# DLRM tower on one core: the opening's index casts, table differences and one-hots in a new order

## The chip, the cores and the metric

The kernel runs on one core of one Trainium2 chip. The metric is the device time of one execution in microseconds, as the median of several runs.

## What is computed

For 2048 samples, 40 embedding rows of 32 values are looked up. Every pair of fields (780 pairs) gets its own 32x32 matrix, and the value of the pair is the bilinear form of the two rows. The 780 values and 16 dense values then go through three dense layers.

```python
e = jnp.stack([tbl_0[ids[:, 0]], tbl_1[ids[:, 1]], ...], axis=1)   # 40 tables of 1000 to 125000 rows
xi = inputs[:, iidx, :]
xj = inputs[:, jidx, :]
out = jnp.einsum('bpd,pde,bpe->bp', xi, bilinear_matrices, xj)
h = jnp.concatenate([z, dense_ctx], axis=1)
h = jnp.maximum(h @ W_top1 + b_top1, 0.0)
h = jnp.maximum(h @ W_top2 + b_top2, 0.0)
y = h @ W_top3
```

## The kernel before

The batch is cut into four blocks of 512 samples. The fields stand in ten chunks of four, and the work of a block is 50 units (a chunk against a chunk, or against itself). A cycle `g` of the main loop is one unit: `project` multiplies a chunk by its matrices on TensorE into the PSUM tile `U` (two halves), `multiply` takes the product with the other chunk on VectorE, and `sum_up` adds over the 32 values on TensorE into `bank_z`. Between these, each cycle carries a few pieces of other work on TensorE (`MISC_AT`): lookups of a coming block, or the dense layers of the last one.

Most fields (24 of 40 in the first two blocks, 28 in the others) are gathered from HBM by GpSimd (`rows`, L589) and turned by a TensorE transpose (L914). The other fields, sixteen in the first two blocks and all of small tables, are looked up without a gather, in four groups of four fields (`GROUPS`, numbered 0 to 3, used in the order 0, 1, 3, 2). A lookup `look(o, q, k)` of block `o` and group `q` has ten steps `k`: VectorE compares the indices with a row number and writes a one-hot tile (`one_hot`, L792), and TensorE multiplies it by that part of the table, 12 matmuls per step, into `misc` (L891). The one-hots live in a ring of five (`ONES`), so that step n+5 waits for TensorE's step n. When ten steps are done, ScalarE copies `misc` away (`keep_look`, L645).

Two things must be made ready for that:

- **Tables.** Each table is split into three bf16 parts. For a group `q`, ScalarE writes the high part (`split_hi`, L606), VectorE the difference (`split_rest`, L772), ScalarE the middle part (`split_mid`, L613), VectorE the last part (`split_low`, L779); each in two halves. `look` waits for the last part.
- **Indices.** The one-hot needs the indices of the group spread over 125 partitions (`idx_wide`, two buffers, jobs alternating). For block 0, group 0, TensorE spreads them by products with an identity (L1004), and ScalarE copies them (L691). For all the others, TensorE turns all 16 index columns (L1012), ScalarE copies them as `idx_T` (L699) and stores them in HBM (`idx_rows`, L702), and the SP queue reads them back to all 125 partitions (`load_wide`, L498).

The SP queue is one list in order of the program. After the index store it reads back the indices of group 1, loads the matrices of step 2 (`load_W(2)`), the tables of group 2, the indices of group 3, `load_W(3)`, the indices of group 2, `load_W(4)` and so on. It stands behind one wait for the store:

```python
sp.wait_ge(idx_stored, 16)
load_wide(0, 1)
load_W(2)
for f in GROUPS[2]:
    load_tab(sp, 2, f)
load_wide(0, 3)
load_W(3)
load_wide(0, 2)
```

Every engine has its own program in order, written by hand; nothing is scheduled by a tool. "The opening" is what runs before the main loop: lookups of groups 0, 1 and 3, and the first two gathered chunks. A program's order of the instructions is fixed, and the engines meet by semaphores alone.

## Time and profile before

| what | value |
|---|---|
| median of 3 runs | 728.96 us (727.7 to 730.28) |
| the profiled execution's own time | 728.67 us |
| its span in the trace | 726.9 us |
| TensorE busy | 693.9 us, 95% of the span |
| VectorE busy | 597.1 us, 82% |
| GpSimd busy | 522.2 us, 72% |
| ScalarE busy | 197.1 us, 27% |

The span is the stretch between the first and the last instruction of the trace; the execution's own time is 1.8 us more. The busy shares are averages over stages with different limits, so the opening has to be read in its own stretches.

### The profile page before, as it was taken

All of it is one profiled execution on the core that took longest, in us unless ns stands there. A gap on an engine that the chain in (4) does not pass through costs nothing.

```text
span 726.9 us, 15700 instructions
## 1 busy us (share of the span) xinstructions
PE 693.9 (95%) x6512; PEld 215.8 (30%) x6512; DVE 597.1 (82%) x608; ACT 197.1 (27%) x309; POOL 522.2 (72%) x631
## 2 busy tenths in 40 slices
PE   2767999999999999999999999999999999999998
PEld 2233333332332232322332232322332222222232
DVE  7989999999986989979876998979967878787800
ACT  3344411422052113043142103143143012213102
POOL 7888888888887888888887888888888887830000
PEclk9999999999999999999999999999999999999999
DMA  4555351222004020000004020000001000000000
GB/s 126 111 89 86 60 99 40 58 52 43 12 12 71 12 40 13 11 12 13 12 12 71 12 35 18 11 12 12 12 12 16 12 12 12 12 8 1 1 1 1
DMA packets 62692, 22.77 MB, mean 31 GB/s; under 512 B 46287, under 2 KB 61805, under 8 KB 62621
## 3 DMA queue, kind: packets, MB, share of 16 engines
q1 hardware_dynamic: 49277, 14.86, 8.8%
q0 software_dynamic: 13312, 6.84, 8.2%
q8 instruction: 51, 0.84, 0.5%
q14 instruction: 20, 0.16, 0.1%
q10 hardware_dynamic: 32, 0.07, 0.1%
HBM read 21.65 MB, written 0.07 MB: 30 GB/s over the span
## 4 chain that ended last, share of the span: by engine, by line
PE 89%; DVE 5%; ACT 4%; DMA 1%; issue 1%; ACTq 0%; DVEq 0%
PE U L940 28%; PE bank_z L965 26%; PE misc L992 14%; PE misc L891 10%; PE U L992 4%; PE U L949 3%; DVE ones L792 3%; PE U L914 3%; ACT x_T L645 1%; DMA idx_wide<-idx_rows 1%; DVE prod L828 1%; ACT x_twin L663 1%; PE bank_z L973 0%; DVE tabs L779 0%; ACT x_twin L666 0%
## 5 line engine op out<-in xcount | busy, mean ns | idle before, releaser
L589 POOL DMA_INDIRECT rows<-in_tbl,idx x416 | 410.2, 986 | 121.3 <-issue 63.5
L828 DVE TENSOR_TENSOR prod<-U,x_T 128x1024 f32<-128x1024 f32 x280 | 329.5, 1216 | 56.5 <-PE U L940 53.7
L965 PE MATMUL bank_z<-prod,select 128*32 128x512 f32 x1600 | 213.1, 604 | 0.7 <-ACT z L625 0.7
L940 PE MATMUL U<-x_T,W 32*128 32x512 f32 x1184 | 187.0, 640 | 7.4 <-ACT x_T L636 3.6
L792 DVE TENSOR_SCALAR ones<-idx_wide,row_of 125x2048 bf16<-125x2048 f16 x140 | 119.0, 872 | 7.0 <-ACT idx_wide L691 3.4
L891 PE MATMUL misc<-ones,tabs 125*32 125x512 bf16 x1680 | 108.4, 388 | 7.3 <-DVE ones L792 5.3
L597 POOL MEMSET pause<- 128x448 uint8 x208 | 111.7, 537 | 0.1
L828 DVE TENSOR_TENSOR prod<-U,x_look 128x1024 f32<-128x1024 f32 x80 | 94.3, 1218 | 21.0 <-PE U L940 18.5
L992 PE MATMUL misc<-z,W 128*32 128x512 f32 x728 | 92.0, 592 | 0.0
L940 PEld LDWEIGHTS U<-x_T,W 32*128 32x128 f32 x1184 | 57.8, 183 | 102.9 <-issue 49.4
L636 ACT ACTIVATE x_T<-U 32x512 f32<-32x512 f32 (+2 forms) x48 | 28.3, 591 | 188.8 <-PE U L914 115.0
L965 PEld LDWEIGHTS bank_z<-prod,select 128*32 128x32 f32 x1600 | 31.6, 107 | 153.5 <-issue 81.4
L891 PEld LDWEIGHTS misc<-ones,tabs 125*32 125x32 bf16 x1680 | 47.4, 98 | 85.0 <-issue 46.0
L625 ACT ACTIVATE z<-bank_z 128x512 f32<-128x512 f32 x28 | 16.7, 598 | 115.8 <-PE bank_z L965 98.7
L940 PE MATMUL U<-x_look,W 32*128 32x512 f32 x256 | 41.8, 640 | 0.0
L645 ACT ACTIVATE x_T<-misc 32x512 f32<-32x512 f32 (+1 forms) x36 | 21.2, 589 | 68.1 <-PE misc L891 67.7
L992 PEld LDWEIGHTS misc<-z,W 128*32 128x32 f32 x728 | 23.6, 110 | 52.7 <-issue 52.7
L992 PE MATMUL misc<-h,W 128*32 128x512 f32 (+1 forms) x204 | 30.4, 593 | 0.8 <-ACT x_T L645 0.8
L663 ACT ACTIVATE x_twin<-x_T 32x512 f32<-32x512 f32 x48 | 30.1, 627 | 1.2
L680 ACT ACTIVATE h<-misc,b 128x512 f32<-128x512 f32 x13 | 8.9, 688 | 64.3 <-PE misc L992 64.3
L949 PE MATMUL U<-x_T,W 32*64 32x512 f32 x160 | 24.1, 612 | 1.2 <-ACT x_twin L673 1.2
L816 DVE TENSOR_TENSOR prod<-U,x_twin 128x1024 f32<-128x1024 f32 x20 | 24.3, 1214 | 0.0
(67 smaller groups left out, 284.1 us busy)
## 6 DMA issues: line engine op xcount, KB each, us to landing
rows<-in_tbl,idx POOLq DMA_INDIRECT x416
idx_wide<-idx_rows SPq DMA_DIRECT2D x13, 500.0 KB
W<-in_W_top SPq DMA_DIRECT2D x100, 8.0 KB
W<-_L_rec_bilinear_matrices SPq DMA_DIRECT2D x72, 16.0 KB, 3.2
prod<-in_tbl SPq DMA_DIRECT2D x4, 156.2 KB
W<-in_W_top SPq DMA_DIRECT2D x35, 2.0 KB
W<-_L_rec_bilinear_matrices SPq DMA_DIRECT2D x4, 128.0 KB
W<-in_W_top SPq DMA_DIRECT2D x1, 512.0 KB
```

The source lines that it names most:

```text
L589: nc.gpsimd.indirect_dma_start(out=rows[:, n % R_SLOTS, t, f, :], out_offset=None, in_=tables[field][:, :], in_offset=bass.IndirectOffsetO ...
L597: nc.gpsimd.memset(pause[:], 0).then_inc(paused, 1)
L636: last = nc.scalar.activation(x_of(o, J)[lo * DIM:hi * DIM, :], U[lo * DIM:hi * DIM, at, 0:N], ACT.Copy)
L645: last = nc.scalar.activation(x_of(o, J)[lo * DIM:hi * DIM, :], misc[s * DIM:(s + hi - lo) * DIM, 0:ROWS[o]], ACT.Copy)
L663: nc.scalar.activation(x_twin[r * DIM:(r + 1) * DIM, 1, 0:N], x_of(o, a + 1)[(CF - 1 - r) * DIM:(CF - r) * DIM, :], ACT.Copy)
L792: nc.vector.tensor_scalar(ones[:, n % ONES, 0:len(fs), 0:N], idx_wide[job % 2][:, 0:len(fs), 0:N], row_of[0:KP, k:k + 1], None, ALU.is_equ ...
L828: last = nc.vector.tensor_tensor(to[:, :, m * N:(m + n) * N].rearrange("p r (m n) -> p r m n", m=n), U[:, at:at + 2, m * N:(m + n) * N].re ...
L891: last = nc.tensor.matmul(misc[s * DIM:(s + 1) * DIM, 0:N], tabs[0:KP, LOOKED.index(field), part, k * DIM:(k + 1) * DIM], ones[:, n % ONES ...
L940: last = nc.tensor.matmul(U[:, at + r % 2, m * N:(m + 1) * N], W[row, at_W:at_W + P], x_of(o, a)[row, :], start=True, stop=True, skip_grou ...
L949: last = nc.tensor.matmul(U[side * P // 2:(side + 1) * P // 2, at + r % 2, m * N:(m + 1) * N], W[row, at_W + side * P // 2:at_W + (side + ...
L965: last = nc.tensor.matmul(bank_z[r * DIM:(r + 1) * DIM, 0:N], sel, prod[:, (2 * g + r // 2) % P_SLOTS, r % 2, m * N:(m + 1) * N], start=(k ...
L992: last = nc.tensor.matmul(bank[part, 0:N], lhs[:, part], rhs, start=(t == 0), stop=(t == depth - 1), skip_group_check=True)
```

## The change

Only the opening changes; no instruction is of a new kind. The indices of group 1 are spread by products on TensorE as those of group 0 are (16 more matmuls and one more copy on ScalarE), and no longer read back from HBM (one SP transfer less). For that, four small casts instead of one stand at the head of VectorE's list, ahead of a memset of `rows`. VectorE makes two one-hots, then the difference of group 0's tables, then the others; the differences of group 3 come behind all ten one-hots of group 1. TensorE turns the 16 index columns after four steps of the first lookup, not ahead of it, so that the copy `idx_T` and the store come after the table copies of group 1. ScalarE zeroes `dense` later, and copies group 3's middle part after `keep_look(0, 1)`, not ahead of it.

```diff
@@ -525,7 +525,6 @@
             for f in GROUPS[3]:
                 load_tab(sp, 3, f)
             sp.wait_ge(idx_stored, 16)
-            load_wide(0, 1)
             load_W(2)
             for f in GROUPS[2]:
                 load_tab(sp, 2, f)
@@ -690,22 +689,24 @@
             act.wait_ge(wide_full, 1)
             nc.scalar.activation(idx_wide[0][:], U[0:KP, 2:2 + CF, :], ACT.Copy).then_inc(wide_made, 1)
 
-            nc.scalar.activation(dense[:].rearrange("p t r d -> p t (r d)"),
-                                 ident[:].unsqueeze(1).to_broadcast([P, SUBS, P]), ACT.Copy, scale=0.0
-                                 ).then_inc(dense_zeroed, 1)
             split_hi(0)
             split_mid(0)
+            act.wait_ge(wide_full, 2)
+            nc.scalar.activation(idx_wide[1][:], U[0:KP, 2:2 + CF, :], ACT.Copy).then_inc(wide_made, 1)
+            split_hi(1)
+            split_mid(1)
             act.wait_ge(idx_T_full, 1)
             nc.scalar.activation(idx_T, U[0:NL, 0:BATCH // NB, :].rearrange("p b n -> p (b n)"), ACT.Copy
                                  ).then_inc(idx_T_made, 1)
             act.wait_ge(idx_T_made, 1)
             act.dma_start(idx_rows[:, :], idx_T).then_inc(idx_stored, 16)
-            split_hi(1)
-            split_mid(1)
+            nc.scalar.activation(dense[:].rearrange("p t r d -> p t (r d)"),
+                                 ident[:].unsqueeze(1).to_broadcast([P, SUBS, P]), ACT.Copy, scale=0.0
+                                 ).then_inc(dense_zeroed, 1)
             keep_look(0, 0)
             split_hi(3)
+            keep_look(0, 1)
             split_mid(3)
-            keep_look(0, 1)
             split_hi(2)
             for g in range(-2, G + 1):
                 if g == 4:
@@ -748,9 +749,6 @@
             nc.vector.tensor_copy(ident_h[:], ident[:]).then_inc(ident_h_made, 1)
             dve.wait_ge(row_of_made, 1)
             nc.vector.tensor_copy(row_of[:], row_of_i[:]).then_inc(row_of_f_made, 1)
-            nc.vector.memset(rows[:, 1:5], 0.0).then_inc(rows_zeroed, 1)
-
-
             beside = [(LOOKED.index(f), f, n) for f, n in ((36, 4), (0, 1), (24, 1), (2, 2), (16, 1), (9, 1), (34, 1),
                                                            (23, 1), (28, 1), (22, 1), (30, 1), (27, 1))]
 
@@ -760,7 +758,8 @@
                 return last
 
             dve.wait_ge(ids_loaded, 16)
-            to_half(0, ROWS[0] // P, beside[:1]).then_inc(idx_h_made, 1)
+            to_half(0, ROWS[0] // P, beside[:4]).then_inc(idx_h_made, 1)
+            nc.vector.memset(rows[:, 1:5], 0.0).then_inc(rows_zeroed, 1)
             for a in range(0, CHUNKS, 2):
                 zero = nc.vector.memset(W[:, w_col(a, a):w_col(a, a) + P], 0.0)
             zero.then_inc(W_zeroed, 1)
@@ -783,10 +782,10 @@
                 N, fs = ROWS[o], GROUPS[q]
                 n, job = LOOK_PART[(o, q, k)], LOOK_ORDER.index((o, q))
                 if k == 0:
-                    if job == 0:
-                        dve.wait_ge(wide_made, 1)
+                    if job < 2:
+                        dve.wait_ge(wide_made, job + 1)
                     else:
-                        dve.wait_ge(wide_landed[job % 2], 16 * ((job + 1) // 2))
+                        dve.wait_ge(wide_landed[job % 2], 16 * (job // 2))
                 if n >= ONES:
                     dve.wait_ge(ones_used, n - ONES + 1)
                 nc.vector.tensor_scalar(ones[:, n % ONES, 0:len(fs), 0:N], idx_wide[job % 2][:, 0:len(fs), 0:N],
@@ -833,32 +832,31 @@
                 last.then_inc(multiplied, 1)
 
             dve.wait_ge(row_of_f_made, 1)
-            for k in range(ONES):
+            for k in range(2):
                 one_hot(0, 0, k)
+            split_rest(0)
+            one_hot(0, 0, 2)
+            split_low(0)
+            one_hot(0, 0, 3)
+            split_rest(1)
             dve.wait_ge(ids_rest_loaded, 16)
-            to_half(ROWS[0] // P, BATCH // P, beside[:1])
-            to_half(0, BATCH // P, beside[1:]).then_inc(idx_h_rest_made, 1)
-            split_rest(0)
-            split_low(0)
-            for k in range(ONES, KC):
+            to_half(ROWS[0] // P, BATCH // P, beside[:4])
+            to_half(0, BATCH // P, beside[4:]).then_inc(idx_h_rest_made, 1)
+            for k in range(4, KC):
                 one_hot(0, 0, k)
-                if k == ONES + 1:
-                    split_rest(1)
-                if k == ONES + 3:
+                if k == 5:
                     split_low(1)
             nc.vector.memset(select[:], 0.0).then_inc(select_zeroed, 1)
             nc.vector.memset(rows[:, 5:7], 0.0).then_inc(rows_zeroed, 1)
             for k in range(KC):
                 one_hot(0, 1, k)
-                if k == ONES:
-                    split_rest(3)
-                if k == ONES + 2:
-                    split_low(3)
+            split_rest(3)
             dve.wait_ge(select_zeroed, 1)
             for s in range(CF):
                 at = CF * (UPT - 1) + s
                 last = nc.vector.memset(select[s * DIM:(s + 1) * DIM, at:at + 1], 1.0)
             last.then_inc(constants, 1)
+            split_low(3)
             for n in HOT_AT[-2]:
                 one_hot(*LOOK_OF_PART[n])
             split_rest(2)
@@ -999,21 +997,25 @@
             pe.wait_ge(ident_h_made, 1)
             pe.wait_ge(idx_h_made, 1)
 
-            for s in range(CF):
-                for t in range(ROWS[0] // P):
-                    last = nc.tensor.matmul(U[0:KP, 2 + s, t * P:(t + 1) * P],
-                                            idx_h[:, t, s:s + 1].to_broadcast([P, KP]), ident_h[:],
-                                            start=True, stop=True, skip_group_check=True)
-            last.then_inc(wide_full, 1)
-            for t in range(BATCH // P):
-                if t == 0:
-                    pe.wait_ge(idx_h_rest_made, 1)
+            for q in (0, 1):
+                if q:
                     pe.wait_ge(wide_made, 1)
-                last = nc.tensor.matmul(U[0:NL, t // SUBS, t % SUBS * P:(t % SUBS + 1) * P], idx_h[:, t, :], ident_h[:],
-                                        start=True, stop=True, skip_group_check=True)
-            last.then_inc(idx_T_full, 1)
+                for s in range(CF):
+                    for t in range(ROWS[0] // P):
+                        last = nc.tensor.matmul(U[0:KP, 2 + s, t * P:(t + 1) * P],
+                                                idx_h[:, t, CF * q + s:CF * q + s + 1].to_broadcast([P, KP]), ident_h[:],
+                                                start=True, stop=True, skip_group_check=True)
+                last.then_inc(wide_full, 1)
             for q in (0, 1):
                 for k in range(KC):
+                    if (q, k) == (0, 4):
+                        pe.wait_ge(idx_h_rest_made, 1)
+                        pe.wait_ge(wide_made, 2)
+                        for t in range(BATCH // P):
+                            last = nc.tensor.matmul(U[0:NL, t // SUBS, t % SUBS * P:(t % SUBS + 1) * P],
+                                                    idx_h[:, t, :], ident_h[:], start=True, stop=True,
+                                                    skip_group_check=True)
+                        last.then_inc(idx_T_full, 1)
                     look(0, q, k)
             pe.wait_ge(constants, 1)
             pe.wait_ge(idx_T_made, 1)
```

The order of VectorE's instructions at the start of its program. `prod`, `W` and `h` are the memory in which the tables of groups 0 and 1, 3, and 2 are staged; `select` is a constant. Before:

```order
L750 CAST row_of<-row_of_i 128x10
L751 MEMSET rows 128x2048
L759 CAST idx_h<-idx 128x4x4
L765 MEMSET W 128x128 x5
L792 TENSOR_SCALAR ones<-idx_wide,row_of 125x2048 x5
L759 CAST idx_h<-idx 128x12x4
L759 CAST idx_h<-idx 128x16 x2
L759 CAST idx_h<-idx 128x16x2
L759 CAST idx_h<-idx 128x16 x8
L772 TENSOR_TENSOR prod<-prod,tabs 125x4x160 x2
L779 TENSOR_TENSOR tabs<-prod,tabs 125x4x160 x2
```

And of the change:

```order
L751 CAST row_of<-row_of_i 128x10
L757 CAST idx_h<-idx 128x4x4
L757 CAST idx_h<-idx 128x4 x2
L757 CAST idx_h<-idx 128x4x2
L762 MEMSET rows 128x2048
L764 MEMSET W 128x128 x5
L791 TENSOR_SCALAR ones<-idx_wide,row_of 125x2048 x2
L771 TENSOR_TENSOR prod<-prod,tabs 125x4x160 x2
L791 TENSOR_SCALAR ones<-idx_wide,row_of 125x2048
L778 TENSOR_TENSOR tabs<-prod,tabs 125x4x160 x2
L791 TENSOR_SCALAR ones<-idx_wide,row_of 125x2048
```

The memset moved behind the first casts, and the difference and the last part of group 0 moved ahead of the third and the fourth one-hot.

The order of ScalarE's instructions from its first copy to the middle part of group 2's tables. The destination `h` is `idx_T`, `tabs<-W` is group 3 and `tabs<-h` is group 2. Before:

```order
L691 ACTIVATE idx_wide<-U 125x2048
L693 ACTIVATE dense<-ident 128x512
L606 ACTIVATE tabs<-prod 125x4x160 x2
L613 ACTIVATE tabs<-prod 125x4x160 x2
L699 ACTIVATE h<-U 16x2048
L702 DMA idx_rows<-h 16x2048
L606 ACTIVATE tabs<-prod 125x4x160 x2
L613 ACTIVATE tabs<-prod 125x4x160 x2
L645 ACTIVATE x_look<-misc 128x512
L606 ACTIVATE tabs<-W 125x4x160 x2
L613 ACTIVATE tabs<-W 125x4x160 x2
L645 ACTIVATE x_T<-misc 32x512 x2
```

And of the change:

```order
L690 ACTIVATE idx_wide<-U 125x2048
L605 ACTIVATE tabs<-prod 125x4x160 x2
L612 ACTIVATE tabs<-prod 125x4x160 x2
L695 ACTIVATE idx_wide<-U 125x2048
L605 ACTIVATE tabs<-prod 125x4x160 x2
L612 ACTIVATE tabs<-prod 125x4x160 x2
L699 ACTIVATE h<-U 16x2048
L702 DMA idx_rows<-h 16x2048
L703 ACTIVATE dense<-ident 128x512
L644 ACTIVATE x_look<-misc 128x512
L605 ACTIVATE tabs<-W 125x4x160 x2
L644 ACTIVATE x_T<-misc 32x512 x2
```

A second copy of `idx_wide` and the table copies of group 1 now stand ahead of the store of the indices.

The order of TensorE's instructions at the start of its program (12 matmuls per lookup step). Before:

```order
L1004 MATMUL U<-ident_h,idx_h 125x128 x16
L1012 MATMUL U<-ident_h,idx_h 16x128 x16
L891 MATMUL misc<-ones,tabs 32x512 x240
L914 MATMUL U<-ident,rows 128x128 x8
L940 MATMUL U<-x_T,W 128x512 x4
```

And of the change:

```order
L1005 MATMUL U<-ident_h,idx_h 125x128 x32
L889 MATMUL misc<-ones,tabs 32x512 x48
L1015 MATMUL U<-ident_h,idx_h 16x128 x16
L889 MATMUL misc<-ones,tabs 32x512 x192
L912 MATMUL U<-ident,rows 128x128 x8
```

The 16 matmuls that turn the index columns moved behind the first four lookup steps.

## Rows read from the trace of the kernel before

**Rows 1.** The page: the span, and TensorE's busy time.

```profile
span 726.9 us, 15700 instructions
...
PE 693.9 (95%) x6512; PEld 215.8 (30%) x6512; DVE 597.1 (82%) x608; ACT 197.1 (27%) x309; POOL 522.2 (72%) x631
```

**Rows 2.** Busy time by stretches: PE, PEld, DVE, ACT, POOL, clock, DMA share, GB/s.

```profile
43.90:47.60 3.70, 3.70 (x43) 1.49 (x44) 1.75 (x4) 1.30 (x2) 3.03 (x3) 0.56 0.91 147
...
70.00:100.00 30.00, 28.84 (x308) 10.01 (x308) 30.00 (x32) 11.18 (x15) 24.51 (x29) 1.00 0.44 73
...
200.00:400.00 200.00, 199.34 (x1888) 61.38 (x1892) 167.10 (x160) 58.78 (x96) 162.53 (x196) 1.00 0.15 25
```

**Rows 3.** Timeline of VectorE, 3 to 70 us: start, busy, what, [idle before].

```profile
4.25 1.76 DVE L751 MEMSET rows<- 128x2048 f32 x1 [0.37 <-issue]
5.93 0.11 DVE L759 CAST idx_h<-idx 128x16 f16<-128x16 int32 x1
...
10.15 3.94 DVE L792 TENSOR_SCALAR ones<-idx_wide,row_of 125x2048 bf16<-125x2048 f16 x5 [3.42 <-ACT idx_wide L691]
14.02 1.15 DVE L759 CAST idx_h<-idx 128x48 f16<-128x48 int32 x12
15.02 1.55 DVE L772 TENSOR_TENSOR prod<-prod,tabs 125x640 f32<-125x640 f32 x2
...
26.25 0.11 DVE L849 MEMSET select<- 128x60 f32 x1
...
27.50 4.61 DVE L792 TENSOR_SCALAR ones<-idx_wide,row_of 125x2048 bf16<-125x2048 f16 x6
...
38.33 4.18 DVE L792 TENSOR_SCALAR ones<-idx_wide,row_of 125x2048 bf16<-125x2048 f16 x5
42.44 1.54 DVE L772 TENSOR_TENSOR z<-h,tabs 125x640 f32<-125x640 f32 x2
...
49.70 2.35 DVE L828 TENSOR_TENSOR prod<-U,x_look 128x1024 f32<-128x1024 f32 x2
51.96 4.05 DVE L792 TENSOR_SCALAR ones<-idx_wide,row_of 125x2048 bf16<-125x2048 f16 x5
```

**Rows 4.** Timeline of ScalarE, 0 to 60 us.

```profile
8.16 1.88 ACT L691 ACTIVATE idx_wide<-U 125x2048 f16<-125x2048 f32 x1 [6.14 <-PE U L1004]
...
10.46 1.35 ACT L606 ACTIVATE tabs<-prod 125x640 bf16<-125x640 f32 x2
15.86 1.47 ACT L613 ACTIVATE tabs<-prod 125x640 bf16<-125x640 f32 x2 [4.06 <-DVE prod L772]
17.24 1.85 ACT L699 ACTIVATE h<-U 16x2048 f16<-16x2048 f32 x1
...
38.93 1.80 ACT L645 ACTIVATE x_T<-misc 32x512 f32<-32x512 f32 x3 [4.58 <-PE misc L891]
```

**Rows 5.** Timeline of TensorE's weight loads, each ahead of four matmuls of a lookup.

```profile
18.34 0.16 PEld L891 LDWEIGHTS misc<-ones,tabs 125*32 125x32 bf16 x4 [0.27 <-issue]
18.77 0.16 PEld L891 LDWEIGHTS misc<-ones,tabs 125*32 125x32 bf16 x4 [0.27 <-issue]
```

**Rows 6.** Timeline of the SP queue's issues, 0 to 45 us.

```profile
21.08 0.27 SPq L498 DMA_DIRECT2D idx_wide<-idx_rows  x1
...
28.21 0.34 SPq L498 DMA_DIRECT2D idx_wide<-idx_rows  x1
...
41.18 0.33 SPq L498 DMA_DIRECT2D idx_wide<-idx_rows  x1
```

**Rows 7.** What the DMA engines moved, in packets, from 28 to 33 us.

```profile
DMA packets 601, 0.65 MB, mean 130 GB/s; under 512 B 81, under 2 KB 601, under 8 KB 601
```

**Rows 8.** The same, from 33 to 38 us.

```profile
DMA packets 1907, 0.71 MB, mean 143 GB/s; under 512 B 1374, under 2 KB 1906, under 8 KB 1906
```

**Rows 9.** Busy time by stretches, as rows 2, of two single microseconds.

```profile
38.00:39.00 1.00, 0.95 (x14) 0.42 (x15) 0.84 (x4) 0.07 (x1) 0.81 (x1) 1.00 0.14 21
...
48.00:49.00 1.00, 1.00 (x24) 0.46 (x20) 0.88 (x2) 0.00 (x0) 1.00 (x1) 1.00 0.32 47
```

## The prediction

> **What bounds the kernel now.** The page comes first: TensorE is busy for 693.9 of 726.9 us [rows 1], so it has 33 us without work. The busy time by stretches says where. From 200 to 400 us TensorE has 199.34 us of 200: nothing is to be had there, and whatever the opening wins, the end gets. From 70 to 100 us VectorE is busy all 30.00 us and TensorE 28.84 [rows 2]. The idle time lies ahead of that, in the opening, which this change rewrites. So I read the opening engine by engine, in the timelines.
>
> VectorE waits 3.42 us for the first copy of the indices and starts its one-hots at 10.15 [rows 3]. The one-hots of group 1 start at 27.50, right behind a memset [rows 3]; their indices, read back from HBM, were asked for at 21.08 [rows 6]. Group 3's one-hots start at 38.33, its successor's (group 2) at 51.96, behind the first two multiplications at 49.70 [rows 3]. ScalarE shows the end of group 1's lookup: `keep_look(0, 1)` starts at 38.93 [rows 4]. From 51.96 on VectorE has all but no gap until 100 us, so I take that start as the mark: what the change moves there, it moves at the end.
>
> **The head start: -1.8 us on VectorE.** The memset of 1.76 us starts at 4.25 after 0.37 us of idle time, so VectorE is free at 3.88 [rows 3]. Now four casts come first: 0.11 us, and three of about 0.1 (1.15 us for 12), so they end at 4.3. From the end of the one cast (6.04) to the first one-hot (10.15) it is 4.1 us today, by TensorE's products and ScalarE's copy [rows 3]; the same again gives 8.4. The memsets of `rows` and `W` fit into that wait.
>
> **VectorE and ScalarE up to the last lookup of group 1.** A one-hot takes 0.79 us (3.94 for five), a pair of table halves 1.55 on VectorE [rows 3], 1.35 (high) or 1.47 (middle) on ScalarE [rows 4]. Two one-hots end at 10.0 and the difference of group 0 at 11.5. ScalarE's middle part begins with its first half at 10.8 and ends at 12.3. The third one-hot ends at 12.3, the first half of the last part at 13.1: TensorE starts its lookups there; today the difference of group 0 alone starts at 15.02 [rows 3]. ScalarE does the second index copy (1.88, [rows 4]) from 12.3 to 14.2 and the high part of group 1 to 15.6; VectorE's difference of it runs from 15.0 to 16.5, the other casts to 17.6, two one-hots to 19.2, group 1's last part to 20.7, four one-hots to 23.8. The two memsets take 1.25 us (26.25 to 27.50, [rows 3]): 25.0. Then ten one-hots of group 1 at 0.76 or so, with no table work between them: 32.7, and one lookup step on TensorE behind it, 33.5. `keep_look(0, 1)` so starts 5.4 us sooner than at 38.93 [rows 4]. That is what the change gets, and two things take from it.
>
> First, ScalarE now has the middle part of group 3 behind it: 1.8 us of `keep_look`, 1.47 of the middle part, 36.8, and VectorE's last part ends 0.8 us behind that, at 37.6. The one-hots of group 3 are wanted at 37.6, just 0.7 us sooner than today.
>
> **The SP queue: +1.8 to +2.8 us.** The second is in a queue that the change hardly touches in the text. The store of the indices now waits for four lookup steps. At the lower clock a step is three groups of matmuls at 0.43 us (18.34 to 18.77, [rows 5]), 1.28 us, so they end at 13.1 + 5.1 = 18.3; the casts that the 16 turning matmuls need end at 17.6. Between the end of those casts (15.17, [rows 3]) and the copy `idx_T` (17.24, [rows 4]) lie 2.1 us of turning at the lower clock; if the clock has doubled by then it is 1.1. The copy starts at 19.4 to 20.4 instead of 17.24. From its start to the first transfer of SP behind the store are 3.84 us (17.24 to 21.08, [rows 4, 6]): 23.2 to 24.2. The transfer that is taken out gives 0.3 us back (0.27 and its gap, [rows 6]). All of SP's list from `load_W(2)` to `load_W(4)` comes 1.8 to 2.8 us later.
>
> When does the transfer of group 3's indices land? It is issued at 28.21 [rows 6]. Its packets are of 1 KB, 500 of them, those of group 2's tables 1.25 KB, 475 of them; packets between 512 B and 2 KB number 520 from 28 to 33 us and 532 from 33 to 38 [rows 7, 8], and from 38 on the traffic is at 21 GB/s [rows 9]. So both follow each other without a gap for ten microseconds, and the indices land at about 37.4 to 38, just ahead of their use at 38.33. With SP's shift this becomes later, less what the tables gain because no read-back for group 1 is ahead of them in the engines (I give 0.6 us back for it, a choice between nothing and the whole). 37.4 + 1.2 to 2.2 is 38.6 to 39.6; I take 39.1. The one-hots of group 3 then start 0.8 us later than today, though all else is ready at 37.6.
>
> **From there to the mark.** Five one-hots (4.11, 38.33 to 42.44), the difference of group 2 (1.5), five one-hots (3.8), the first multiplication (2.26, 49.70 to 51.96) [rows 3]: 39.1 + 11.7 = 50.8. Today it is 51.96: after 42.44 + 1.5 + 3.8 = 47.7 the multiplication should start, and starts at 49.70, since TensorE began this lookup late; those 1.9 us of waits go, as TensorE now begins at about 40. Group 2's indices are issued at 41.18, and from 48 the traffic is at 47 GB/s [rows 6, 9]; with the shift they land by about 50.8 at the latest, at the mark. They cost nothing, or a few tenths at the late end. The sum is 50.8 - 51.96, **-1.2 us**, between -0.7 and -1.7 by the two ends of the landing. The profiled execution's own time is 728.67, so 727.5; the median of the runs shown is 0.3 above it, so I say 727.8, and the times below are made against the median too.
>
> **Edits at nothing.** Zeroing `dense` (0.6 us on ScalarE) goes into a gap of ScalarE ahead of `keep_look(0, 0)`; without it it would delay that copy by 0.6. GpSimd's gathers do not depend on the order. SP's matrices are later by 2 us, and those whose issue ends by 44 us (`load_W(3)`) are used several cycles into the main loop. 16 more matmuls fall into TensorE's wait at 8 us.
>
> **A rule against the row.** Today TensorE stands still ahead of the first `project`, and from 43.9 to 47.6 us its granted clock is 0.56, mostly the lower level of 1.2 GHz [rows 2]. The changed kernel has a longer wait there, from 33.5 to 39, with 1 us of transposes in it, and the lookups behind it trickle as VectorE feeds them, so the lower clock may hold for all ten steps. Then TensorE ends them at 40 + 12.8 = 52.8 and VectorE is held up behind: about -0.5 us are left instead of -1.2. The Trainium skill (TensorE: Matmul & The Clock Gate, section "Loop structure matters more than you think") has it that waits between matmuls turn the array cold; by that rule the sum would be -0.5, by the row, in which the clock came back after 3.7 us, -1.2.
>
> **Rivals.**
> 1. Forecast, -1.2 us: the landing of group 3's indices decides. 0.45.
> 2. The transfer is hidden: it lands by 37.6, since SP's issues or the tables take less time with the engines empty before them. Group 1's took 6.4 us from its issue to a one-hot at 27.50, and by that figure this one would be there at 30.5 + 6.4 = 36.9. Against it: the tables are ahead of it, and 975 packets at some 105 per us need 9.3 us. 11.7 us from 37.6 is 49.3: -2.7 us, 726.3. 0.20.
> 3. The lower clock holds for the whole lookup: -0.5, 728.5. 0.12.
> 4. The gain is made and lost again behind the mark, as TensorE and VectorE, both all but full until 100 us, fall out of step: 0, 729.0. 0.15.
> 5. Slower. The tables of group 0 haven't landed at 8.4. ScalarE came to them at 10.46 [rows 4], so nothing shows that they were there before. If they land late, everything up to the store shifts, and with it both the need and the landing. A landing of group 3's indices past 40.3 makes the kernel slower, by 1 us for each; for that the tables would have to come at 9.6 or later, and for 0.3% at 11.8, which is past 10.46 where they were in use. At 10.46 it is 729.9. A further microsecond or two of SP's issues would add to it: 731. 0.08.
>
> **How the numbers follow.** 0.3% is 2.2 us, about what a measurement of this kernel can tell from no change. In this count cases 1, 3 and 4 lie within it, case 2 just beyond it on the fast side, case 5 around its edge on the slow side. Faster by over 0.3%: most of case 2 and a tail of case 1, 0.26. Slower: the far half of case 5 and a rest for what I haven't seen, 0.08. Within: 0.66. The range takes in cases 1 to 4 and the near half of 5: 725.8 to 729.9. The forecast's own range is 727.3 to 728.3.
>
> **What the changed profile would show.** The first one-hot at 8.4; TensorE's first lookup at 13.1; `idx_T` at 19.4 to 20.4 and SP's next issue at 23.2 to 24.2; `keep_look(0, 1)` at 33.5; VectorE idle for 1 to 2 us ahead of group 3's one-hots with the read-back as the cause, and their start near 39.1; the first one-hot of group 2 near 50.8. If that idle time is missing and the start is at 37.6, case 2 holds. The forecast is wrong too if the 16 matmuls or the casts come out twice as long, or if the engines lose the lead between 51 and 100 us.

## The result

The changed kernel takes 727.18 us (median of 20 executions, 725.44 to 730.95), the kernel before 730.89 (20 executions, 727.7 to 733.18) on the same chip. The ratio is 0.9959, with a 95% interval of 0.9944 to 0.9974: 3.0 us less, between 1.9 and 4.1. The profiled execution took 726.81 us, 1.9 less than that of the kernel before.

The page of the changed kernel, the rows that answer to [rows 1]:

```profile
span 725.0 us, 15735 instructions
...
PE 697.4 (96%) x6528; PEld 217.9 (30%) x6528; DVE 595.4 (82%) x611; ACT 198.9 (27%) x310; POOL 517.2 (71%) x631
```

VectorE's timeline of the changed kernel, against [rows 3]:

```profile
8.37 1.71 DVE L791 TENSOR_SCALAR ones<-idx_wide,row_of 125x2048 bf16<-125x2048 f16 x2 [1.36 <-ACT idx_wide L690]
...
24.51 7.80 DVE L791 TENSOR_SCALAR ones<-idx_wide,row_of 125x2048 bf16<-125x2048 f16 x10
...
35.84 1.63 DVE L778 TENSOR_TENSOR tabs<-W,tabs 125x640 bf16<-125x640 f32 x2 [1.74 <-ACT tabs L612]
38.82 3.99 DVE L791 TENSOR_SCALAR ones<-idx_wide,row_of 125x2048 bf16<-125x2048 f16 x5 [1.35 <-DMA idx_wide<-idx_rows]
...
50.31 3.94 DVE L791 TENSOR_SCALAR ones<-idx_wide,row_of 125x2048 bf16<-125x2048 f16 x5
...
56.61 0.75 DVE L791 TENSOR_SCALAR ones<-idx_wide,row_of 125x2048 bf16<-125x2048 f16 x1 [0.89 <-PE misc L889]
...
61.06 2.33 DVE L827 TENSOR_TENSOR prod<-U,x_look 128x1024 f32<-128x1024 f32 x2
```

The first one-hot comes at 8.37, group 1's at 24.51 without a wait, and group 3's at 38.82 after 1.35 us of waiting for their read-back. The first one-hot of group 2, the mark of the prediction, comes at 50.31, 1.65 us sooner than the 51.96 of before. Then the one-hots at 56.61 and behind it wait for TensorE, and the multiplication of cycle 1 starts at 61.06. In the kernel before that was 61.57: of 1.65 us only 0.5 is left there.

ScalarE's and the SP queue's timelines show the steps in between:

```profile
19.03 1.87 ACT L699 ACTIVATE h<-U 16x2048 f16<-16x2048 f32 x1 [1.80 <-PE U L1015]
...
33.25 1.79 ACT L644 ACTIVATE x_T<-misc 32x512 f32<-32x512 f32 x3 [7.02 <-PE misc L889]
```

```profile
23.72 3.65 SPq L491 DMA_DIRECT2D W<-_L_rec_bilinear_matrices  x8
27.40 1.44 SPq L454 DMA_DIRECT2D h<-in_tbl  x4
28.89 0.80 SPq L498 DMA_DIRECT2D idx_wide<-idx_rows  x1
```

The copy `idx_T` starts at 19.03 (17.24 before), the list behind the store at 23.72 (21.08), `keep_look(0, 1)` at 33.25 (38.93).

The loss behind the mark is in the clock (the experiments test this). Busy time by stretches of the changed kernel (length of the stretch, then PE, PEld, DVE, ACT, POOL, granted clock, DMA share, GB/s), single microseconds:

```profile
39.00:40.00 1.00, 1.00 (x8) 0.00 (x0) 1.00 (x2) 0.38 (x1) 1.00 (x2) 0.50 0.22 37
...
56.00:57.00 1.00, 1.00 (x16) 0.45 (x12) 0.39 (x1) 0.51 (x1) 0.73 (x2) 0.50 0.73 144
```

A clock of 0.50 is the lower level, 1.2 GHz. The kernel before has one stretch at it up to 70 us, from 44.4 to 47.8, most of which lies in the 0.56 of [rows 2]. The changed one has two, 38.3 to 41.7 and 51.9 to 58.7, each at the end of a wait of TensorE (3.11 us up to 38.35) or just behind one (1.95 us up to 51.55). The ends of a stretch are worked out from the microseconds at its ends: 0.63 from 38 to 39, for instance, is 0.26 us at the upper level and the rest at the lower one.

### The profile page after: what moved, and what is told of

It reads as the page before. It is cut to its first block, busy times and chain, and to the rows that moved or that the text cites. A ratio compares the mean times of both kernels' runs of the same rounds, so it can differ in the third digit from the quotient of the medians.

```text
span 725.0 us, 15735 instructions
## 1 busy us (share of the span) xinstructions
PE 697.4 (96%) x6528; PEld 217.9 (30%) x6528; DVE 595.4 (82%) x611; ACT 198.9 (27%) x310; POOL 517.2 (71%) x631
## 4 chain that ended last, share of the span: by engine, by line
PE 89%; DVE 5%; DMA 2%; issue 1%; ACT 1%; SPq 0%; DVEq 0%
PE U L938 29%; PE bank_z L963 27%; PE misc L990 14%; PE misc L889 10%; PE U L990 4%; PE U L947 3%; PE U L912 3%; DVE ones L791 3%; DMA idx_wide<-idx_rows 1%; DVE prod L827 1%; DMA prod<-in_tbl 1%; ACT x_T L644 1%; PE bank_z L971 0%; SPq L454 0%; DVE prod L771 0%
## 5 line engine op out<-in xcount | busy, mean ns | idle before, releaser
L791 DVE TENSOR_SCALAR ones<-idx_wide,row_of 125x2048 bf16<-125x2048 f16 x140 | 117.2, 861 | 4.5 <-PE misc L889 1.8
L889 PE MATMUL misc<-ones,tabs 125*32 125x512 bf16 x1680 | 110.5, 393 | 8.3 <-DVE ones L791 3.8
L596 POOL MEMSET pause<- 128x448 uint8 x208 | 108.6, 522 | 0.1
L912 PE MATMUL U<-ident,rows 128*128 128x128 f32 x144 | 23.4, 286 | 0.9 <-DVE select L857 0.9
L815 DVE TENSOR_TENSOR prod<-U,x_twin 128x1024 f32<-128x1024 f32 x20 | 24.2, 1211 | 0.0
```

Source lines behind the costliest of these rows:

```text
L596: nc.gpsimd.memset(pause[:], 0).then_inc(paused, 1)
L791: nc.vector.tensor_scalar(ones[:, n % ONES, 0:len(fs), 0:N], idx_wide[job % 2][:, 0:len(fs), 0:N], row_of[0:KP, k:k + 1], None, ALU.is_equ ...
L889: last = nc.tensor.matmul(misc[s * DIM:(s + 1) * DIM, 0:N], tabs[0:KP, LOOKED.index(field), part, k * DIM:(k + 1) * DIM], ones[:, n % ONES ...
L912: last = nc.tensor.transpose(U[:, at, t * P:(t + 1) * P], rows[:, n % R_SLOTS, t].rearrange("p f d -> p (f d)"), ident[:])
```

## The experiments

In each table "group 3", "mark" and "multiply" are the starts (us) of group 3's one-hots, of the first one-hot of group 2 and of the multiplication of cycle 1 in the profiled execution. For the kernel before they are 38.33, 51.96 and 61.57, for the changed one 38.82, 50.31 and 61.06. The theories: A, the landing of group 3's read-back (the transfer that brings their indices from HBM) holds the opening; B, the lower clock of TensorE behind it does.

### The changed kernel again, the read-back first, the gaps filled, the memset first

The changed kernel once more:

> The changed kernel once more, as the measure for its neighbours and to see how far one profiled execution repeats. Theory A (the lead is made in the opening, and the body passes it on): first one-hot of group 2 at 50.3 us again, and all of the difference to the kernel before that stands at 91 us (1.1 us in the first profile) stands at the end too, but for scatter of the body. Rival (the body itself gives back or wins something through its phase): the difference grows from 1.1 to 1.9 us at the same place as in the first profile, between 461 and 488 us. Both: a ratio of 0.996 to the kernel before.

The read-back of group 3 as the first transfer behind the store:

```diff
             sp.wait_ge(idx_stored, 16)
+            load_wide(0, 3)
             load_W(2)
             for f in GROUPS[2]:
                 load_tab(sp, 2, f)
-            load_wide(0, 3)
```

> The read-back of group 3's indices is the first transfer behind the store, ahead of load_W(2) and of group 2's tables. Theory A (the landing of this read-back decides): VectorE's idle 1.35 us ahead of group 3's one-hots goes, they start at 37.5, the first one-hot of group 2 comes at 49.0 instead of 50.3, and the kernel takes 1.3 us less than the changed one. Rival B (the lower clock of TensorE around 52 to 58 us sets the end of the opening): the first one-hot of group 2 comes sooner, but the one-hots behind it wait longer for TensorE, and the kernel takes the same time as the changed one, within 0.4 us. Rival C: group 2's tables now come late, ScalarE waits for them ahead of its high part (36.3 in the changed kernel), and it is slower by up to 2 us.

TensorE's gaps filled:

```diff
+            def idle_products(n):
+                for _ in range(n):
+                    nc.tensor.matmul(bank_z[:, 0:P], ident_h[:], ident_h[:], start=True, stop=True, ...)
...
+            idle_products(12)
             pe.wait_ge(constants, 1)
...
                     project(g + 1)
+                if g == 0:
+                    idle_products(24)
...
                     turn(o, c)
+                if g < 0:
+                    idle_products(48 if g == -2 else 30)
```

> The changed kernel with matmuls of no use (128x128, into a bank that is not in use yet) in TensorE's gaps: 12 behind the lookup of group 1, 48 behind the first transposes, 30 behind the third, 24 behind project(1). Nothing else is touched. Rival B (the clock): the granted clock stays at 1.0 from 38 to 60 us, the five one-hots behind group 2's last part don't wait for TensorE (1.8 us of waits in the changed kernel), the multiplication of cycle 1 starts at 59.9 instead of 61.06, and the kernel takes about 1.2 us less. Theory A alone (only the read-back counts): no difference within 0.4 us. If the filling matmuls themselves come in the way, up to 1 us more.

The memset back ahead of the first casts:

```diff
+            nc.vector.memset(rows[:, 1:5], 0.0).then_inc(rows_zeroed, 1)
             beside = [...]
...
             to_half(0, ROWS[0] // P, beside[:4]).then_inc(idx_h_made, 1)
-            nc.vector.memset(rows[:, 1:5], 0.0).then_inc(rows_zeroed, 1)
```

> The changed kernel with the memset of rows (1.76 us) back ahead of the first casts. Theory A: the first one-hot at 10.1 instead of 8.37, the store 1.7 us later, with it the read-back of group 3's indices, the first one-hot of group 2 at 52.0, and the kernel takes 1.7 us more than the changed one. Rival (the head start is lost in later waits anyway): within 0.4 us of the changed one.

| kernel | ratio to before (95%) | median us | group 3 | mark | multiply |
|---|---|---|---|---|---|
| changed, again | 0.9949 (0.9926 to 0.9972) | 727.49 | 38.13 | 49.78 | 61.61 |
| read-back first | 0.9938 (0.9915 to 0.9961) | 725.47 | 37.55 | 48.98 | 59.61 |
| gaps filled | 0.9944 (0.9920 to 0.9967) | 725.96 | 38.29 | 49.49 | 59.01 |
| memset first | 0.9972 (0.9952 to 0.9992) | 727.8 | 40.00 | 51.19 | 62.39 |

VectorE's rows of the read-back first: no wait is left ahead of group 3.

```profile
37.55 3.93 DVE L791 TENSOR_SCALAR ones<-idx_wide,row_of 125x2048 bf16<-125x2048 f16 x5
...
48.98 3.95 DVE L791 TENSOR_SCALAR ones<-idx_wide,row_of 125x2048 bf16<-125x2048 f16 x5
55.00 0.75 DVE L791 TENSOR_SCALAR ones<-idx_wide,row_of 125x2048 bf16<-125x2048 f16 x1 [0.60 <-PE misc L889]
```

The mark is where theory A had it (49.0). The tables of group 2, now issued behind the read-back, don't come late (rival C): ScalarE takes them at 36.50, with no wait, and at 36.34 in the changed kernel. VectorE's rows of the filled kernel:

```profile
49.49 3.96 DVE L791 TENSOR_SCALAR ones<-idx_wide,row_of 125x2048 bf16<-125x2048 f16 x5
55.16 3.93 DVE L791 TENSOR_SCALAR ones<-idx_wide,row_of 125x2048 bf16<-125x2048 f16 x5 [0.25 <-PE misc L889]
59.01 2.34 DVE L827 TENSOR_TENSOR prod<-U,x_look 128x1024 f32<-128x1024 f32 x2
```

The read-back is as late as in the changed kernel's own repeat (38.29 against 38.13), and the mark is within 0.3 us of it (49.49 against 49.78). The way from the mark to the multiplication shrinks to 9.52 us, from 10.75 in the first profile of the changed kernel and 11.83 in the second, and the waits of the five one-hots from 1.83 to 0.25. The clock has 1.00 from 38 to 60 us, as theory B had it. So both theories hold, each for its own stretch: A to the mark, B behind it. The medians of both lie 1.5 to 2 us below the changed kernel's, but the intervals of the ratios overlap, so of each edit alone the time is not shown, only the place in the trace. From the mark on, the read-back first has still 10.63 us to the multiplication: it moves the mark and leaves the clock's loss as it is.

The repeat of the changed kernel tells how far one profile goes. Its mark is 0.5 us sooner, but its multiplication is at 61.61, where the kernel before had 61.57: of the lead nothing is left there. It has one more stretch at the lower clock (rows by stretches, as above):

```profile
60.00:70.00 10.00, 9.06 (x95) 3.08 (x88) 8.72 (x9) 0.07 (x1) 8.00 (x11) 0.81 0.56 88
```

The same stretch of the first profile has a clock of 1.00. The memset costs 1.4 us at the mark (51.19 against 49.78) where 1.7 was expected; at the end it is 1.7 us by the ratios and 0.3 by the medians, with overlapping intervals, so its price in time is not shown.

### Both edits together, one part of the change at a time, and a dose

Both edits, with 24 more filling matmuls between the halves of `project(2)`:

> Both edits of the first set together, the read-back of group 3 first and the gaps of TensorE filled with matmuls of no use, with 24 more of them between the two halves of project(2) and 34 instead of 24 behind project(1), since in the first filled kernel the clock fell at 61 to 65 us. If the landing of the read-back (theory A) and the lower clock (theory B) are two separate costs, they add: first one-hot of group 2 at 48.6 to 49.0 us, no stretch at the lower clock from 38 to 70 us, the multiplication of cycle 1 at 58.2 (59.61 with the read-back first alone, 59.01 filled alone), the kernel about 1 us below the read-back first alone, and its executions closer together than the 3 us between the clusters of the others. If only one of the two counts, it is as fast as the faster of the two.

Only the products for group 1 and the four small casts that they need, on the kernel before:

```diff
-            load_wide(0, 1)
...
             nc.scalar.activation(idx_wide[0][:], U[0:KP, 2:2 + CF, :], ACT.Copy).then_inc(wide_made, 1)
+            act.wait_ge(wide_full, 2)
+            nc.scalar.activation(idx_wide[1][:], U[0:KP, 2:2 + CF, :], ACT.Copy).then_inc(wide_made, 1)
...
-            to_half(0, ROWS[0] // P, beside[:1]).then_inc(idx_h_made, 1)
+            to_half(0, ROWS[0] // P, beside[:4]).then_inc(idx_h_made, 1)
...
```

> The kernel before with one part of the change alone: group 1's indices spread by products (16 more matmuls, the second copy on ScalarE straight behind the first), no read-back of them; the order of everything else as before. By the reading of the profile of before, where VectorE came to group 1's one-hots at 27.42 and the indices were there, this part gives nothing of itself: group 1's one-hots at 27.5 +-0.4, the store of the indices at 21.1 +-0.4, the first one-hot of group 2 at 51.9 +-0.5, and the time of the kernel before within 0.1%. Rival (the products are what gains): most of the change's 0.4 to 0.5% is here.

All but the products:

```diff
             sp.wait_ge(idx_stored, 16)
+            load_wide(0, 1)
             load_W(2)
...
-            act.wait_ge(wide_full, 2)
-            nc.scalar.activation(idx_wide[1][:], U[0:KP, 2:2 + CF, :], ACT.Copy).then_inc(wide_made, 1)
```

> The changed kernel without its products for group 1: their indices are read back from HBM again, first behind the store; everything else in the new order. Theory A: the store is still behind four lookup steps, so the indices of group 1 land 6.4 us behind 23.4, at about 29.8, where VectorE wants them at 24.6; the idle time of 5 us goes through to the first one-hot of group 2, at about 54.5 to 55, 3 us later than in the kernel before, and the kernel is 2 to 3 us slower than before. Rival (the later waits swallow it): no slower than the kernel before.

The read-back of group 3 later in SP's list (`load_W` takes the first and the last of its transfers here):

```diff
-            load_wide(0, 3)
-            load_W(3)
+            load_W(3, 0, 6)
+            load_wide(0, 3)
+            load_W(3, 6)
```

> The changed kernel with the read-back of group 3's indices behind the first six of the 18 transfers of load_W(3): a dose of about 4 us of SP issues at the place that theory A names. Theory A: group 3's one-hots start 3 to 4 us later than 38.1 to 38.8, VectorE idle ahead of them by as much, the first one-hot of group 2 at 53 to 54, the kernel 2.5 to 4 us slower than the changed one. Rival B (the clock sets the end of the opening, a landing later by this much is hidden): under 1 us.

| kernel | ratio to before (95%) | median us | group 3 | mark | multiply |
|---|---|---|---|---|---|
| first and filled | 0.9915 (0.9895 to 0.9935) | 724.68 | 37.34 | 48.76 | 58.27 |
| products only | 0.9982 (0.9964 to 0.9999) | 730.1 | 37.98 | 52.10 | 64.05 |
| all but the products | 1.0021 (1.0004 to 1.0038) | 732.63 | 43.01 | 54.21 | 66.42 |
| read-back late | 0.9975 (0.9955 to 0.9994) | 729.11 | 38.75 | 50.18 | 61.42 |

The two costs add: the multiplication comes at 58.27 (58.2 was expected), the clock is at its upper level throughout, and the kernel is 0.85% or 6.2 us below the one before, the best of all. One part of the expectation is missed: its six executions are not closer together than those of the others (723.18 to 726.61). The interval of its ratio (to 0.9935) lies below the changed kernel's of 20 executions (from 0.9944) and overlaps that of its repeat (from 0.9926). By stretches, this kernel, where the changed one has a clock of 0.77 from 38 to 60:

```profile
38.00:60.00 22.00, 19.94 (x294) 11.04 (x296) 21.75 (x28) 10.10 (x17) 18.24 (x21) 1.00 0.52 89
```

Without the products the new order is worse than the old. VectorE's row of that kernel:

```profile
29.31 8.51 DVE L790 TENSOR_SCALAR ones<-idx_wide,row_of 125x2048 bf16<-125x2048 f16 x10 [4.90 <-DMA idx_wide<-idx_rows]
```

The wait of 4.90 us was expected as 5, the mark (54.21) was expected at 54.5 to 55, and the kernel is 1.5 us slower than before, a bit less than the 2 to 3 expected. The products alone leave the mark at 52.10, as expected, though SP's list behind the store starts at 22.61 and not at the expected 21.1 (`idx_T` starts at 17.64, 0.4 us later than before, and from there to SP's first transfer it is 4.97 us instead of 3.84). Their ratio is 0.18% below 1, its interval just clear of it, where nothing was expected. So neither part alone gives what both give: the late store needs the products, and the products need the new order.

The dose is the miss. The SP row of that kernel, and VectorE's:

```profile
32.24 0.34 SPq L498 DMA_DIRECT2D idx_wide<-idx_rows  x1
```

```profile
38.75 3.94 DVE L792 TENSOR_SCALAR ones<-idx_wide,row_of 125x2048 bf16<-125x2048 f16 x5 [1.14 <-DMA idx_wide<-idx_rows]
```

The issue is 3.35 us later than in the first profile of the changed kernel, and the one-hots start no later (38.75 against 38.82). But SP's whole list stands 0.65 us sooner in this profile. In both profiles of the changed kernel, in the filled one and in the one with the memset first, group 3's one-hots start 9.9 to 10.0 us behind the end of SP's issues of group 2's tables (28.84 and 38.82, for instance); here it is 10.55 (28.20 and 38.75). So a read-back issued 4 us later behind the tables costs 0.6 us and not 3 to 4: it is hardly the moment of the issue that holds this transfer. The kernel is 0.16% to 0.26% slower than the changed one by the ratios, with overlapping intervals.

What the DMA engines moved in the changed kernel, from 28 to 33 and from 33 to 38 us:

```profile
DMA packets 633, 0.58 MB, mean 116 GB/s; under 512 B 196, under 2 KB 632, under 8 KB 632
```

```profile
DMA packets 1618, 0.76 MB, mean 152 GB/s; under 512 B 1004, under 2 KB 1618, under 8 KB 1618
```

436 and 614 packets of 512 B to 2 KB, 1050 in ten microseconds, in a row, as in the kernel before (1052, [rows 7, 8]). With the later issue there is a gap in the row, from 33 to 34 us:

```profile
DMA packets 448, 0.10 MB, mean 101 GB/s; under 512 B 395, under 2 KB 448, under 8 KB 448
```

53 such packets in that microsecond, with 100 in the one ahead of it and 120 in the one behind. By the counts the tables' packets go first, up to 33 us, and the read-back's behind them; issued at 32.24 it came just as they ended. The trace doesn't name the transfer of a packet, so this is read from the counts. It fits that issue and one-hots are 6.5 us apart here, and 6.2 for group 1's read-back in the kernel without the products (issued at 23.10 ahead of everything, one-hots at 29.31). So the dose was too small for its question: it used up the time that the read-back spends behind the tables, and a still later issue would have to show. In the first set the read-back was issued at 23.70, ahead of the tables; 515 such packets moved from 24 to 29 us and 38 in the next microsecond, so it was through at about 29.5 (an estimate from these counts), long before VectorE wanted it.

### Group 3's tables early

The table work of group 3 in its old place, alone and with the read-back first:

```diff
-            keep_look(0, 1)
             split_mid(3)
+            keep_look(0, 1)
...
                 one_hot(0, 1, k)
-            split_rest(3)
+                if k == ONES:
+                    split_rest(3)
+                if k == ONES + 2:
+                    split_low(3)
...
-            split_low(3)
```

> The changed kernel with the table work of group 3 back where it was: VectorE's difference and last part among the one-hots of group 1 (behind the sixth and the eighth), ScalarE's middle part ahead of keep_look(0, 1). Theory A: VectorE is ready for group 3's one-hots at about 36.2 us, but their indices land at 38.1 to 38.8 as in the changed kernel, so they start there; the lookup of group 1 ends 3 us later on TensorE, project(0) starts at about 40; the first one-hot of group 2 comes at 50.3 to 51, and the kernel is at the changed one's time, up to 0.8 us slower. Rival (moving these tables is a gain of its own, by the shorter lookup of group 1): 2 us or more slower.

> The same, with the read-back of group 3's indices first behind the store. Theory A: the one-hots of group 3 start at 36.2 (37.5 with the read-back first in the new table order), but the sixth must wait until TensorE has used the first, and TensorE starts this lookup only at about 41, at the lower clock: one step per 1.28 us. The first one-hot of group 2 comes at about 50.5 instead of 48.98, and the kernel is 1 to 2 us slower than with the read-back first alone. Rival (VectorE's order alone counts): the first one-hot of group 2 at 47.7 and 1 us faster.

> The changed kernel again, as the measure on the same chip for the kernel beside it. The two kernels of the last set ran on a chip on which the kernel before takes 807 us, so their times can't be held against the earlier ones. Both theories: 0.995 to 0.996 of the kernel before if the chip is one like the first two, and the same order of its opening (first one-hot of group 2 at 49.8 to 50.3 us).

> The changed kernel with the table work of group 3 back where it was, again. Its opening on the slower chip reached the first one-hot of group 2 at 50.04, as theory A had it (50.3 to 51). Theory A: the time of the changed kernel beside it within 0.15%, up to 1 us slower. Rival: 2 us or more slower.

| kernel | ratio to before (95%) | before, us | group 3 | mark | multiply |
|---|---|---|---|---|---|
| tables 3 early | 0.9994 (0.9959 to 1.0028) | 806.86 | 37.77 | 50.04 | 61.04 |
| the same, read-back first | 1.0015 (0.9978 to 1.0052) | 806.86 | 35.90 | 50.95 | 62.68 |
| changed, third time | 1.0019 (0.9996 to 1.0042) | 801.61 | 38.74 | 50.18 | 62.21 |
| tables 3 early, again | 0.9996 (0.9967 to 1.0024) | 801.61 | 37.82 | 52.02 | 63.87 |

In these two sets every kernel takes 70 to 76 us more, the kernel before too. The opening of the changed kernel reaches the mark at the same place to a few tenths (50.18), but by another way: its one-hots of group 3 start without a wait, right behind group 3's last part, for which VectorE waited.

```profile
37.26 1.56 DVE L778 TENSOR_TENSOR tabs<-W,tabs 125x640 bf16<-125x640 f32 x2 [2.79 <-ACT tabs L612]
```

Here `keep_look(0, 1)` started at 34.68 and not at 33.25, so the tables and not the read-back held the start in this profile. Most of the time is lost behind the opening. The busy time of this profile (span 799.4 us) from 70 us on, beside the same of the second profile:

```profile
70.00:800.00 730.00, 700.93 (x5968) 209.47 (x5960) 539.72 (x513) 169.21 (x270) 467.73 (x565) 0.98 0.13 21
```

```profile
70.00:727.00 657.00, 651.31 (x5956) 197.63 (x5954) 535.56 (x512) 169.15 (x270) 463.00 (x564) 1.00 0.14 23
```

The instructions are the same, and there are 29 us without work for TensorE where there were 6, and 50 us more in which it is shown busy. The clock of 0.98 is a part of it: by it some 29 us are at the lower level, which can cost up to 15 us (an estimate from the row). I can't say why the rest; most of these waits have no releaser in the trace. In these sets the opening's lead doesn't show in the time: the changed kernel is at 1.0019 there, its interval just touching 1 and well above 0.9974. That the body, no longer full, swallows the lead is argued; no profile of the kernel before was taken there.

For the edits themselves the times of these sets decide nothing, and the traces little. With the read-back first and the tables early, VectorE starts group 3's one-hots at 35.90, but the sixth comes only at 43.76; it needs a place in the ring, and TensorE begins this lookup at 42.24. The mark is 50.95, where the read-back first in the new table order has 48.98, so theory A's mechanism is in the trace. Its size is not: the kernel with the tables early and the read-back in its place has the mark at 50.04 in one profile and at 52.02 in the other, with the changed kernel at 50.18, so 2 us at the mark are no more than what two profiles of one kernel differ by. What putting group 3's tables later is worth stays open.

## Why the prediction came out as it did

**What bounds it, and the mark.** Right for this pair of profiles. VectorE's first one-hot of group 2 carried the change, and every term up to it was close: 8.4 foreseen and 8.37 measured, TensorE's first lookup 13.1 and 12.99, `idx_T` 19.4 to 20.4 and 19.03 (just below), SP 23.2 to 24.2 and 23.72, `keep_look(0, 1)` 33.5 and 33.25, VectorE ready for group 3 at 37.6 and 37.5, the landing 39.1 and 38.8, the mark 50.8 and 50.31. The sum was -1.2 and the mark says -1.65. The rest is one-hots and turning matmuls that took a few tenths less: the 16 that turn the columns took 1.1 us, where the kernel before had 1.9 (the prediction took both as possible). I called this a doubled clock; it is read from the durations alone, since the rows of the granted clock have 1.00 in both traces from the start up to there.

**The SP queue.** The size was right and its step wrong. I let the landing follow SP's issues by 1.8 to 2.8 us. The dose shows that an issue 4 us later behind the same tables costs 0.6 us. The way from the copy `idx_T` to SP's first transfer was put at 3.84 us, from one profile; it is 4.69 in the first profile of the changed kernel and 4.29 in the second, and 3.84 is the shortest of all profiles here. `idx_T` came sooner by about as much, so SP's 23.72 fits by luck in part. The landing was right in the sum because the tables move with the store: the landing goes with their issue, 9.9 to 10.0 us behind it.

**The clock.** Of the two values in the prediction, "-0.5" and "-1.2", the first profile has the first at 61 us (61.06 against 61.57), and the repeat nothing (61.61). It did not come as the rival had it, so the agreement with "-0.5" is luck. The lookup of group 3 was fed in time (its low stretch ended at 41.7, and at 43.3 in the repeat), and a second low stretch at 51.9 to 58.7, which I hadn't foreseen, slowed the lookup of group 2. The filled kernel shows it: 1.2 us of the way from the mark to the multiplication are the clock's against the first profile, 2.3 against the repeat. The Trainium skill (TensorE: Matmul & The Clock Gate, section "Loop structure matters more than you think") has it that with a long wait between matmuls the array goes cold. The trace agrees, at a place where I didn't apply it: TensorE waited 1.95 us ahead of the second stretch and 1.75 us in it.

**From the mark to the end.** Here the size failed. "What the change moves there, it moves at the end" gave -1.2 us or, from the measured mark, -1.65; the time moved by 3.0 (1.9 to 4.1), beyond the 0.3% that I thought the likeliest. That the time itself, 727.18, lies so near the 727.8 of the forecast is luck: the kernel before took 730.89 in this comparison and not the 728.96 from which I subtracted. ScalarE's copies of `bank_z`, the same work in each kernel, show the lead on its way (us of their start):

| copy | before | changed | changed, again | read-back first | filled | first and filled |
|---|---|---|---|---|---|---|
| first | 91.34 | 90.23 | 92.44 | 88.79 | 89.88 | 88.01 |
| 18th | 488.12 | 486.01 | 487.93 | 484.64 | 486.86 | 484.83 |
| last | 697.19 | 695.30 | 697.25 | 693.95 | 695.81 | 694.13 |

The same kernel, changed and changed again, is 2.2 us apart at the first copy and 1.95 at the last. The lead of the first profile grows from 1.1 to 1.9 us on the way. The growth is at one place, as the rival in the expectation of the repeat had it: from the 17th to the 18th copy it is 27.15 us in the profiles of the kernel before and of the filled one, and 26.33 to 26.35 in the other profiles of this table. So one profiled pair can't give this difference to a microsecond, and the one that I worked from was at the short end. Its mean clock was 0.998; none of the 60 executions of the kernel before in the first and the second set had more than 0.995, and their times go with it:

| mean clock of the kernel before | 0.988 | 0.991 | 0.993 | 0.995 |
|---|---|---|---|---|
| first set: mean us (executions) | 733.1 (5) | 732.4 (13) | 731.2 (7) | 728.8 (8) |
| second set: mean us (executions) | 732.7 (6) | 731.4 (7) | 730.9 (8) | 729.5 (6) |

So the execution that was profiled spent less time at the lower level than any of the 60. Where the usual one has them, no profile of the kernel before shows. The nearest is the kernel with the products only, whose order is the old one: at a mean clock of 0.991 it has the mark at 52.10, but the multiplication at 64.05 and the first copy of `bank_z` at 94.87, 3.5 us behind the 91.34 of the kernel before. The two profiles of the changed kernel are 2.4 and 4.6 us ahead of that at the first copy, and 2.4 and 4.3 at the last; the measured 3.0 lies between. That the kernel before loses in the same way is argued, not shown. It isn't all either: the executions of the kernel with both edits all have a clock of 1.0 and still lie at 723.2 to 723.7 and at 725.6 to 726.6. What makes these 2 to 3 us stays open.

So the step that was mis-sized is the last one, the move from the mark to the end at no cost. From the mark to the first copy alone the profiles of the first two sets and of this result lie between 39.3 us (both edits, no low stretch) and 43.4 us (without the products), and the three longest (42.7 us and more) have some 10 us at the lower level behind the mark, the others at most 7.

**The rivals.** The hidden transfer (2) didn't come: the wait of 1.35 us is in the trace. The late tables (5) neither, ScalarE took them at 8.15. The body (4) took nothing back in the result and the first set, where the lead at the last copy is no smaller than at the first. In the last two sets, with the body 70 to 76 us longer, the lead doesn't show at the end.

## What to carry to other kernels

In an opening where several engines hand over to each other, follow the change through the queue that it hardly touches: a store that comes later moves all that is listed behind it. Ask of a late transfer what is ahead of it in the DMA engines before its issue; here a place ahead of 0.6 MB of tables was worth 0.8 to 1.3 us at the mark, and an issue 4 us later behind them cost 0.6. And look at the granted clock in each gap of TensorE: a gain of a microsecond in a wait can be spent on matmuls at half the clock, and matmuls of no use in the gaps can give it back (114 of them here). Before a mark in one profile is taken for the end, look at the mean clock of the other executions: here the profiled one had a mean clock that none of 60 others reached.

## What the runs showed of the hardware

- The stretches at 1.2 GHz move from execution to execution of one kernel: 38.3 to 41.7 and 51.9 to 58.7 us in the first profile of the changed kernel, 36.4 to 43.3, 53.5 to 60.3 and 63.8 to 67.2 in the second. With 114 matmuls in the gaps none was left up to 60 us and one at 62 to 65; with 34 more and the read-back first there was none.
- Executions of one kernel differ in their mean clock and, with it, in their time: 728.8 us at 0.995 and 733.1 at 0.988 for the kernel before in the first set.
- With a read-back in packets of 1 KB behind tables in packets of 1.25 KB, from HBM to 125 partitions, the engines moved 1050 packets of 512 B to 2 KB in ten microseconds where the read-back was issued at 28.89, and 1042 where it was issued at 32.24; a few of them belong to other transfers.
- In two of the four sets all kernels of this case have medians of 801.6 to 807.1 us instead of 724.7 to 732.6, at mean clocks of 0.960 to 0.985 instead of 0.986 to 1.0, though the opening of the changed kernel reaches its mark at the same place (50.18 us). The second and the fourth set are recorded on chips of the same number (2), with 731.06 and 801.61 us for the kernel before, so that number doesn't tell them apart.
